# Second stage of a vision tower kernel: patch sums in four column groups, last network product by quarters, key-value sums earlier

## The chip, the cores and the metric

The kernel runs on one core of a Trainium2 chip. The core's engines are PE (TensorE, matmuls from the on-chip memory SBUF into the accumulators PSUM), DVE (VectorE), ACT (ScalarE), POOL (GpSimd) and SP (which here only issues DMA transfers). They run on their own and meet at semaphores. The metric is the device time of one execution in microseconds, the median of several runs. The profile is one further execution, taken with the hardware profiler.

## The reference

```python
def _performer(x, kqv_w, kqv_b, pw, pb, g1, b1, g2, b2, m1w, m1b, m2w, m2b, w):
    h = _ln(x, g1, b1)
    k, q, v = jnp.split(h @ kqv_w.T + kqv_b, 3, axis=-1)
    kp = _prm_exp(k, w)                      # exp(w k - |k|^2 / 2) / sqrt(m), m = 32
    qp = _prm_exp(q, w)
    D = jnp.einsum('btm,bm->bt', qp, kp.sum(axis=1))[..., None]
    kptv = jnp.einsum('btn,btm->bnm', v, kp)
    y = jnp.einsum('btm,bnm->btn', qp, kptv) / (D + EPS)
    y = v + (y @ pw.T + pb)
    h2 = _ln(y, g2, b2)
    return y + jax.nn.gelu(h2 @ m1w.T + m1b, approximate=False) @ m2w.T + m2b

t = _unfold3(x, 1)          # 4 images, 3 channels, 224 x 224: 27 values a token
t = _performer(t, p1...)    # first stage, 50176 tokens of 64 channels an image
t = _unfold3(t, 2)          # 3 x 3 patches with stride 2: 576 values a token
t = _performer(t, p2...)    # second stage, 12544 tokens an image
t = _unfold3(t, 2) @ proj   # 3136 tokens of 768 channels, then a state space layer
...                         # and a layer of experts (the tail)
```

All is in fp32. The change is in the second `_performer`.

## The kernel before

The program has three stages one after the other, with a barrier between: `performer1`, `performer2` (the second stage) and `tail`. Each engine's program is written out by hand as a loop; every engine works its instructions off in that order and waits on semaphores (`after(eng, s, n)` is such a wait that is left out for n of 0 or less).

In the second stage a unit is 448 tokens (4 output rows of 112), 28 units an image, 112 in all. A pair of units is a slot's work: 56 pairs, n = 0 to 55, and the loops run n = 0 to 65. The two units of a pair lie on the two halves of the 128 partitions (64 channels each). The 3 x 3 patches are never written out: the convolutions read strided rows of `xt` and `x4`, and the layer norm over a patch comes in by a mean and a variance that are computed apart.

The first pass over a pair n: SP loads its rows (`load_x`, up to three pairs ahead). ACT squares them (`squares` into `xs`). POOL adds both over the patch's columns and row pairs (`sums`, into `cs` and `css`). PE adds them over the partitions in `statistics` (lines 912 to 922): four matmuls with a constant matrix, the sums of the two units into the two halves of bank 3 (line 917), those of the squares into bank 4 (line 920), 64 columns of the array each, so that every one of 64 partitions holds the same mean. ACT squares the mean from bank 3 into `ms` (line 1113), DVE takes it from bank 4 (line 1228: the variance), ACT makes the inverse deviation `rs` of it by Ln and Exp (lines 1119, 1121). PE convolves to keys and queries (`conv_kq`) and values (`conv_v`), lines 929, 932 and 937; DVE multiplies with `rs` (1238, 1250). One slot later follow `logits` (965, 968), the features (ACT, 1079 and 1083), `transposes` (979, 984), DVE's copy `vt` (1245), and `keys_values` (990): features times values, which DVE adds up over the image in `kvacc` (1263). At the start of an image's second pass `operands`, `matrix` (997, 998) and `weights` make of it the matrices `dw`, `ycw` and `yw`; the latter two are masked by `pm2s` and `pm2` (line 1188) so that a product with the queries picks out the right unit of four. `pm2s` is `pm2` with the two units of the upper 64 partitions (64 to 127) exchanged.

The second pass goes over quads of four units (two pairs; 7 an image, 28 in all, q = 0 to 27), in banks 6 and 7 (`quad_banks`; for some quads of the last image 0 and 1). It has five stages (`second`): 0 the denominator (1022; DVE adds, inverts and multiplies the queries, 1198 to 1202), 1 the centred y (1010, 1004; DVE copies it as `yc`, 1207; ACT squares it, `ycs`, 1091), 2 its variance (1004; ACT Ln and Exp, 1095, 1097), 3 the network's first product (1004; DVE scales, 1212; ACT gelu, 1100), 4 y again (1010) and the network's last product (line 1038), which DVE adds up with a bias and the values as `ob` (line 1217); SP stores it (829). `quads_due` sets when: stages 0 and 1 in one slot, 2, 3 and 4 in the next. So from slot 16 on the even slots hold stages 0 and 1, the odd ones 2 to 4, of the image before; the third image's last quad falls in slots 56 and 57, and the seven quads of the last image in slots 58 to 65, in twos and the last alone, with no convolutions beside them.

A matmul with 64 x 64 weights uses a quarter of the array, one with 128 x 64 half of it, and matmuls on different parts can go side by side. `quadrants` (lines 1000 to 1006) issues four with 64 x 64 weights; for the second of two banks the halves are exchanged (`half[r ^ p]`), so that all four parts of the array are in use.

PE's order in a slot, from line 1041 on: `statistics(n)`, `logits(n - 1)`, at an image's start `matrix`, stages 0 and 2, `conv_kq(n)`, stage 3, `transposes(n - 1)`, `conv_v(n)`, stages 1 and 4, `keys_values(n - 1)`. DVE's: `operands`, variance, `weights`, stage 0, the product `kq`, stage 3, the copy `vt`, the values `vp`, stages 1 and 4, the sum `kvacc`. ACT's: `ms`, features, Ln and Exp of `rs`, `squares(2n + 3)`, stage 2, squares of `kq`, stage 3, `squares(2n + 4)`, stage 1.

Of the kernel before, what the change touches and what calls it, by code (L numbers as in the profile page):

```python
# [21 lines left out]
T = 448  # L22
# [620 lines left out]
def performer2(nc, sem, w, c, t1, t2):  # L643

    with ExitStack() as ctx:
# [15 lines left out]
        def both(q):  # L661
# [8 lines left out]
        bd32 = sb("bd32b", [128, 4, 32])  # L670
        pm2 = sb("pm2", [128, 2, 64])
        pm2s = sb("pm2s", [128, 2, 64])
# [66 lines left out]
                 (srep, c["srep"]), (jb, c["jb64"]), (bd32, c["bd32"].rearrange("p (a m) -> p a m", a=4)),  # L739
                 (pm2, c["pm2"]), (pm2s, c["pm2s"]), (c64, c["c64"]), (c64bd, c["c64bd"]), (c64dup, c["c64dup"]),  # L740
                 (eps64, c["eps64"]), (wa, w["wa2"]), (wb, w["wb2"]), (wf2, w["wf2"]), (ga, w["ga2"]),
# [139 lines left out]
        def _(pe):  # L881
# [30 lines left out]
            def statistics(n):  # L912
                after(pe, s_va, n)
                after(pe, s_vt, n - 1)
                pe.wait_ge(s_cs, 2 * n + 2)
                for g in range(2):
                    mm(ps[half[g], 3, 0:T], ones576[:, 0:64], cs[:, (2 * n + g) % 4, 0:TR2, :], start=True, stop=True)
                pe.wait_ge(s_css, 2 * n + 2)
                for g in range(2):
                    last = mm(ps[half[g], 4, 0:T], ones576[:, 0:64], css[:, (2 * n + g) % 4, 0:TR2, :],  # L920
                              start=True, stop=True)
                last.then_inc(s_st, 1)
# [90 lines left out]
            def second(stage, q):  # L1013
# [20 lines left out]
                if stage == 4:  # L1034
                    pe.wait_ge(s_gl, q + 1)
                    from_q(q, yw)
                    for p in range(2):
                        last = mm(bank(quad_banks(q) + p), m2[:, :], gl[:, u, p, :], start=False, stop=True)
                    last.then_inc(s_o, 1)

            for n in range(LAST):
                if n < NP:
                    statistics(n)
                if 1 <= n <= NP:
                    logits(n - 1)
                if n > BP and n % BP == 1 and n <= NP + 1:
                    matrix(n // BP - 1)
                for stage, q in quads_due(n, (0, 2)):
                    second(stage, q)
                if n < NP:  # L1050
                    conv_kq(n)
                for stage, q in quads_due(n, (3,)):
                    second(stage, q)
                if 1 <= n <= NP:
                    transposes(n - 1)
                if n < NP:
                    conv_v(n)
                for stage, q in quads_due(n, (1, 4)):
                    second(stage, q)
                if 1 <= n <= NP:  # L1060
                    keys_values(n - 1)

        @block.scalar
        def _(act):
# [43 lines left out]
            for n in range(LAST):  # L1108
                u = n % 2
                if n < NP:  # L1110
                    act.wait_ge(s_st, n + 1)
                    after(act, s_va, n - 1)
                    fn(ms[:, u, :], bank(3), ACT.Square).then_inc(s_ms, 1)
                if 1 <= n <= NP:
                    features(n - 1)
                if n < NP:
                    act.wait_ge(s_va, n + 1)
                    after(act, s_vn, n - 1)
                    fn(rs[:, u, :], ms[:, u, :], ACT.Ln, bias=eps64[:, :]).then_inc(s_lv, 1)
                    act.wait_ge(s_lv, n + 1)  # L1120
                    fn(rs[:, u, :], rs[:, u, :], ACT.Exp, scale=-0.5).then_inc(s_rs, 1)
                    squares(2 * n + 3)
# [18 lines left out]
        def _(dve):  # L1141
# [42 lines left out]
            def weights(b):  # L1184
                dve.wait_ge(s_mp, b + 1)
                ts(kps[:, b % 2:b % 2 + 1], ps[:, 2, 128:129], 1.0 / M, None, ALU.mult).then_inc(s_kps, 1)
                for dst, lo, mask in ((ycw, 64, pm2s), (yw, 0, pm2)):
                    nc.vector.scalar_tensor_tensor(dst[:, b % 2], ps[:, 2, lo:lo + 64].unsqueeze(1)
                                                   .to_broadcast([128, 2, 64]), 1.0 / M, mask[:, :, :], ALU.mult,
                                                   ALU.mult).then_inc(s_yw, 1)  # L1190
# [3 lines left out]
            def second(stage, q):  # L1194
# [18 lines left out]
                if stage == 4:  # L1213
                    at = 2 * q % RV
                    dve.wait_ge(s_o, q + 1)
                    after(dve, s_t2[u], 64 * (q // 2))
                    nc.vector.scalar_tensor_tensor(ob[:, u], both(q), bo[:, :], vp[:, at:at + 2, :], ALU.add,
                                                   ALU.add).then_inc(s_ob, 1)

            for n in range(LAST):  # L1220
# [5 lines left out]
                if n < NP:  # L1226
                    dve.wait_ge(s_ms, n + 1)
                    tt(ms[:, u, :], bank(4), ms[:, u, :], ALU.subtract).then_inc(s_va, 1)
                if first:
# [16 lines left out]
                if n < NP:  # L1246
# [3 lines left out]
                    tt(vp[:, n % RV, :], bank(2), rs[:, u, :], ALU.mult).then_inc(s_vn, 1)  # L1250
                for stage, q in quads_due(n, (1, 4)):
                    second(stage, q)
                if 1 <= n <= NP:
# [3 lines left out]
                    for g in range(2):  # L1257
# [3 lines left out]
                        else:  # L1261
                            dve.wait_ge(s_kva, 2 * (n - 1))
                            tt(kvacc[half[g], b % 2, :], kvacc[half[g], b % 2, :], kv, ALU.add).then_inc(s_kva, 1)


# [1065 lines left out]
```

## Time and profile before

| | us |
|---|---|
| median of 3 runs | 8061.27 (8054.65 to 8067.14) |
| the profiled execution's own time | 8056.0 |
| its span | 8054.2 |
| first stage | 0 to about 1784 |
| second stage, 56 slots with convolutions | about 1831 to 2971 |
| second stage, the last eight quads | 2971 to about 3110 |
| tail | about 3113 to 8054 |

| engine | busy us of the span | share |
|---|---|---|
| PE | 7205.3 | 89% |
| DVE | 6156.8 | 76% |
| POOL | 5546.6 | 69% |
| ACT | 4377.1 | 54% |

Busy shares over the whole span mix three stages. To read the second stage, take windows inside it, then the timeline of one odd and one even slot: where a row begins, and which row of another engine ended just before. The rows' ends of matmuls are modelled and overlap the next start, so distances between starts are used for PE.

### The profile page before, as it was taken

What the parts mean: (1) busy time and instruction counts of PE and PEld (TensorE: products, weight loads), DVE (VectorE), ACT (ScalarE), POOL (GpSimd) and SP (SyncE); (2) the same over time, 40 slices, a digit from 0 to 9 for tenths busy, and PEclk for the clock granted to TensorE, in tenths of its full rate; (3) what the DMA queues carried; (4) which work ended last, traced back from release to release, by engine and by line L of the source; (5) the groups of instructions that cost most, each with busy time, mean ns of one, the idle gap of its engine ahead of it and who ended that gap; (6) DMA issues with size and microseconds to landing.
All of it is one profiled execution on the core that took longest, in us unless ns stands there. A gap on an engine that the chain in (4) does not pass through costs nothing.

```text
span 8054.2 us, 87036 instructions
## 1 busy us (share of the span) xinstructions
PE 7205.3 (89%) x31060; PEld 2876.3 (36%) x31060; DVE 6156.8 (76%) x6517; ACT 4377.1 (54%) x7837; POOL 5546.6 (69%) x2487
## 2 busy tenths in 40 slices
PE   8999999979999995689889898898888988988888
PEld 6444444323443431133333333333333333333323
DVE  2566666761333333999999999999999999999995
ACT  3566666763344442555555555555555555555553
POOL 0011111128766640999999999999999999999994
PEclk9999999989999997799899999899998999989988
DMA  1111111125545423333333333333334333334331
GB/s 40 33 46 45 42 44 43 42 60 114 105 98 109 100 61 84 101 116 113 131 130 125 112 119 125 126 124 126 119 109 136 122 128 113 117 128 132 125 110 56
DMA packets 358649, 786.32 MB, mean 98 GB/s; under 512 B 72229, under 2 KB 284727, under 8 KB 350729
## 3 DMA queue, kind: packets, MB, share of 16 engines
q1 hardware_dynamic: 320838, 689.44, 29.1%
q0 software_dynamic: 21712, 51.75, 2.5%
q10 hardware_dynamic: 15666, 39.57, 1.4%
q8 instruction: 246, 4.03, 0.2%
q14 instruction: 187, 1.52, 0.1%
HBM read 597.06 MB, written 183.35 MB: 97 GB/s over the span
## 4 chain that ended last, share of the span: by engine, by line
DVE 34%; issue 13%; ACT 7%; PE 6%; POOL 1%; DMA 0%; DVEq 0%; SPq 0%; ACTq 0%
DVE v L2052 16%; DVE v L2061 15%; ACT ps L1935 2%; PE ps L1672 2%; DVE dl L2042 1%; PE ps L1674 1%; PE ps L1667 1%; ACT dl L1880 1%; ACT gm L1964 1%; PE ps L1802 1%; PE ps L1681 1%; PE ps L1736 1%; ACT dl L1885 0%; ACT L1965 0%; ACT L1964 0%
## 5 line engine op out<-in xcount | busy, mean ns | idle before, releaser
L2061 DVE TENSOR_TENSOR_SCAN v<-ps,v 128x901 f32<-128x901 f32 x1344 | 2732.3, 2033 | 93.4 <-DVE v L2052 0.9
L1636 POOL TENSOR_TENSOR v<-v,ct 128x1792 f32<-128x1792 f32 x672 | 2258.2, 3360 | 288.8 <-ACT st L1896 285.6
L1624 POOL TENSOR_TENSOR v<-xr,bt 128x1792 f32<-128x1792 f32 x672 | 2258.2, 3361 | 65.8 <-DMA bt<-bc_rows 65.8
L1935 ACT ACTIVATE ps<-dr,aa 128x448 f32<-128x448 f32 x2688 | 1596.0, 626 | 1087.4 <-DVE v L2061 1077.7
L2052 DVE SCALAR_TENSOR_TENSOR v<-ps,aa,v 128x448 f32<-128x448 f32 x2688 | 1686.2, 669 | 11.5 <-ACT ps L1935 5.4
L236 POOL DMA_DIRECT2D tokens<-ob x448 | 235.3, 532 | 1533.5 <-DVE ob L563 1490.5
L1736 PE MATMUL ps<-v,dg 128*32 128x448 f32 x5376 | 779.3, 617 | 476.9 <-POOL v L1636 251.8
L1802 PE MATMUL ps<-w_or_w,gm 128*112 128x384 f32 x1792 | 692.4, 534 | 67.8 <-DVE gm L2127 65.0
L1896 ACT ACTIVATE st<-v 128x4 f32<-128x4 f32 x672 | 140.7, 209 | 912.5 <-DVE v L2061 910.6
L1672 PE MATMUL ps<-x,wpa 128*128 128x448 f32 x1008 | 479.0, 613 | 85.9 <-ACT h L1859 75.1
L1667 PE MATMUL ps<-h,w_or_w 128*128 128x448 f32 x1344 | 538.3, 551 | 9.7 <-DVE bcs L2036 9.7
L1802 PEld LDWEIGHTS ps<-w_or_w,gm 128*112 128x112 f32 x1792 | 331.3, 193 | 439.8 <-issue 121.6
L1674 PE MATMUL ps<-x,wpb 64*128 64x448 f32 x1008 | 450.5, 578 | 0.0
L1736 PEld LDWEIGHTS ps<-v,dg 128*32 128x32 f32 x5376 | 136.1, 113 | 856.7 <-POOL v L1636 375.1
L929 PE MATMUL ps<-xt,wa 128*64 128x448 f32 x2016 | 435.0, 565 | 0.0
L552 DVE COPY ht<-ps 112x512 f32<-112x512 f32 x112 | 77.4, 691 | 466.6 <-ACT kp L433 466.6
L1667 PEld LDWEIGHTS ps<-h,w_or_w 128*128 128x128 f32 x1344 | 251.4, 192 | 294.0 <-issue 264.5
L1238 DVE TENSOR_TENSOR kq<-ps,rsa 128x896 f32<-128x896 f32 x56 | 61.1, 1092 | 358.7 <-PE ps L937 337.5
L586 DVE RECIPROCAL qpn<-qpn 128x448 f32<-128x448 f32 x112 | 330.7, 2953 | 3.8
L1672 PEld LDWEIGHTS ps<-x,wpa 128*128 128x128 f32 x1008 | 190.9, 201 | 338.8 <-issue 230.5
L290 PE MATMUL ps<-wki,h 128*112 128x256 f32 x896 | 277.3, 391 | 1.9 <-DVE hu L544 1.9
L1674 PEld LDWEIGHTS ps<-x,wpb 64*128 64x128 f32 x1008 | 174.7, 186 | 271.0 <-issue 271.0
(331 smaller groups left out, 11534.1 us busy)
## 6 DMA issues: line engine op xcount, KB each, us to landing
xr<-h_by_channel SPq DMA_DIRECT2D x168, 896.0 KB, 5.0
dr<-delta_by_channel SPq DMA_DIRECT2D x168, 896.0 KB, 4.7
x<-tokens SPq DMA_DIRECT2D x252, 224.0 KB, 5.3
tokens<-ob POOLq DMA_DIRECT2D x448, 112.0 KB, 2.4
w_or_w<-in_w SPq DMA_DIRECT2D x29, 1536.0 KB, 6.4
w_or_w<-centred_w SPq DMA_DIRECT2D x27, 1536.0 KB, 9.1
h_by_channel<-h SPq DMA_DIRECT2D x112, 336.0 KB, 5.1
delta_by_channel<-dl SPq DMA_DIRECT2D x224, 168.0 KB, 2.8
```

The costliest lines, as they stand in the source:

```text
L586: nc.vector.reciprocal(qpn[:, u % 3, :], qpn[:, u % 3, :]).then_inc(s_dr, 1)
L929: mm(ps[half[g], o, 0:T], wa[:, j, cols], xt[:, 2 * (n % 3) + g, 0:TR2, j:j + 2 * S2 - 1:2], start=(j == 0), stop=False)
L1624: tt(v[:, n % RING, :, 2:T + 2], xr[:, dc % 2, :].rearrange("p (i t) -> p i t", i=4), bt[:, q:q + 1, :].to_broadcast([128, 4, T]), ALU.mul ...
L1636: tt(v[:, n % RING, :, 2:T + 2], v[:, n % RING, :, 2:T + 2], ct[:, q:q + 1, :].to_broadcast([128, 4, T]), ALU.mult).then_inc(s_cm, 1)
L1667: last = mm(into, weights(dc), h[:, i % 3, dc, :], start=(dc == 0), stop=(dc == DC - 1))
L1672: mm(into, even(j), x3[:, 0:TR3, j:j + 2 * S3 - 1:2], start=(j == 0), stop=False)
L1674: return mm(into, odd(j - 3), x3[0:64, 1:TR3 + 1, j - 3:j - 4 + 2 * S3:2], start=False, stop=(j == 5))
L1736: last = mm(ps[32 * g:32 * g + 32, YB, 0:T], dg[:, 4 * k + g, :], v[:, n % RING, g, 2:T + 2], start=(q == 0), stop=False)
L1802: mm(into[:, 0:D // 2], gm[:, m, cs], w2[:, m, lo:lo + D // 2], start=(m == 0), stop=False)
L1935: fn(decay(g), dr[:, dc % 2, g, :], ACT.Exp, scale=aa[:, 4 * k + g:4 * k + g + 1]).then_inc(s_a, 1)
L2052: stt(row, decay(g), aa[:, 4 * k + g:4 * k + g + 1], row, ALU.subtract, ALU.mult).then_inc(s_wt, 1)
L2061: nc.vector.tensor_tensor_scan(row, flat[:, 1024 * pair + 1:1024 * pair + GW + T + 2], row, 0.0, ALU.mult, ALU.add).then_inc(s_sc, 1)
```

## The change

Three things, all in the second stage:

- `statistics` waits for both sums first and then issues its four matmuls with 32 columns each, into the four quarters (32 partitions each) of bank 3: the means of the two units in partitions 0 to 31 and 32 to 63, the means of squares in 64 to 95 and 96 to 127. ACT's square and DVE's difference work on 64 partitions, and ACT's Ln is issued four times, 32 partitions each, to spread the two variances over the 128 partitions of `rs`; the Exp waits for all four.
- The network's last product goes by `quadrants` with the 64 x 64 blocks of `m2` (which is block-diagonal) in place of two matmuls with 128 x 128. Its second bank so holds the two units on exchanged halves; `yw` is masked with `pm2s` to match, `pm2` and its load are gone, and DVE adds up `ob` in three instructions in place of one: 448 elements on 128 partitions for the first bank, then twice 448 on 64 partitions for the second.
- `keys_values(n - 1)` on PE and the sum `kvacc` on DVE stand ahead of stages 1 and 4 in the slot, not behind.

```diff
--- before.py
+++ after.py
@@ -668,7 +668,6 @@
         srep = sb("srep2", [128, 128])
         jb = sb("jb64b", [128, 128])
         bd32 = sb("bd32b", [128, 4, 32])
-        pm2 = sb("pm2", [128, 2, 64])
         pm2s = sb("pm2s", [128, 2, 64])
         c64 = sb("c64", [64, 64])
         c64bd = sb("c64bd", [128, 128])
@@ -737,7 +736,7 @@
 
         loads = [(ident, c["ident"]), (ones576, c["ones576"]), (sqk, c["sqk"]), (dd64, c["dd64"]),
                  (srep, c["srep"]), (jb, c["jb64"]), (bd32, c["bd32"].rearrange("p (a m) -> p a m", a=4)),
-                 (pm2, c["pm2"]), (pm2s, c["pm2s"]), (c64, c["c64"]), (c64bd, c["c64bd"]), (c64dup, c["c64dup"]),
+                 (pm2s, c["pm2s"]), (c64, c["c64"]), (c64bd, c["c64bd"]), (c64dup, c["c64dup"]),
                  (eps64, c["eps64"]), (wa, w["wa2"]), (wb, w["wb2"]), (wf2, w["wf2"]), (ga, w["ga2"]),
                  (gb, w["gb2"]), (ba, w["ba2"]), (bb, w["bb2"]), (kqb, w["kqb2"]), (vb, w["vb2"]), (pb, w["pb2"]),
                  (pw, w["pw2"]), (prj[:, 0:64], w["pwt2"]), (m1, w["m1bd2"]), (m2, w["m2bd2"]), (g2, w["g22"]),
@@ -913,12 +912,12 @@
                 after(pe, s_va, n)
                 after(pe, s_vt, n - 1)
                 pe.wait_ge(s_cs, 2 * n + 2)
-                for g in range(2):
-                    mm(ps[half[g], 3, 0:T], ones576[:, 0:64], cs[:, (2 * n + g) % 4, 0:TR2, :], start=True, stop=True)
                 pe.wait_ge(s_css, 2 * n + 2)
-                for g in range(2):
-                    last = mm(ps[half[g], 4, 0:T], ones576[:, 0:64], css[:, (2 * n + g) % 4, 0:TR2, :],
-                              start=True, stop=True)
+                for k, data in enumerate((cs, css)):
+                    for g in range(2):
+                        at = 64 * k + 32 * g
+                        last = mm(ps[at:at + 32, 3, 0:T], ones576[:, 0:32], data[:, (2 * n + g) % 4, 0:TR2, :],
+                                  start=True, stop=True)
                 last.then_inc(s_st, 1)
 
             def taps(n, o):
@@ -1034,9 +1033,7 @@
                 if stage == 4:
                     pe.wait_ge(s_gl, q + 1)
                     from_q(q, yw)
-                    for p in range(2):
-                        last = mm(bank(quad_banks(q) + p), m2[:, :], gl[:, u, p, :], start=False, stop=True)
-                    last.then_inc(s_o, 1)
+                    quadrants(q, m2, lambda p, r: gl[half[r], u, p, :], False).then_inc(s_o, 1)
 
             for n in range(LAST):
                 if n < NP:
@@ -1055,10 +1052,10 @@
                     transposes(n - 1)
                 if n < NP:
                     conv_v(n)
+                if 1 <= n <= NP:
+                    keys_values(n - 1)
                 for stage, q in quads_due(n, (1, 4)):
                     second(stage, q)
-                if 1 <= n <= NP:
-                    keys_values(n - 1)
 
         @block.scalar
         def _(act):
@@ -1110,14 +1107,16 @@
                 if n < NP:
                     act.wait_ge(s_st, n + 1)
                     after(act, s_va, n - 1)
-                    fn(ms[:, u, :], bank(3), ACT.Square).then_inc(s_ms, 1)
+                    fn(ms[half[0], u, :], ps[half[0], 3, 0:T], ACT.Square).then_inc(s_ms, 1)
                 if 1 <= n <= NP:
                     features(n - 1)
                 if n < NP:
                     act.wait_ge(s_va, n + 1)
                     after(act, s_vn, n - 1)
-                    fn(rs[:, u, :], ms[:, u, :], ACT.Ln, bias=eps64[:, :]).then_inc(s_lv, 1)
-                    act.wait_ge(s_lv, n + 1)
+                    for at in range(0, 128, 32):
+                        of = slice(at // 64 * 32, at // 64 * 32 + 32)
+                        fn(rs[at:at + 32, u, :], ms[of, u, :], ACT.Ln, bias=eps64[of, :]).then_inc(s_lv, 1)
+                    act.wait_ge(s_lv, 4 * (n + 1))
                     fn(rs[:, u, :], rs[:, u, :], ACT.Exp, scale=-0.5).then_inc(s_rs, 1)
                     squares(2 * n + 3)
                 for stage, q in quads_due(n, (2,)):
@@ -1184,7 +1183,7 @@
             def weights(b):
                 dve.wait_ge(s_mp, b + 1)
                 ts(kps[:, b % 2:b % 2 + 1], ps[:, 2, 128:129], 1.0 / M, None, ALU.mult).then_inc(s_kps, 1)
-                for dst, lo, mask in ((ycw, 64, pm2s), (yw, 0, pm2)):
+                for dst, lo, mask in ((ycw, 64, pm2s), (yw, 0, pm2s)):
                     nc.vector.scalar_tensor_tensor(dst[:, b % 2], ps[:, 2, lo:lo + 64].unsqueeze(1)
                                                    .to_broadcast([128, 2, 64]), 1.0 / M, mask[:, :, :], ALU.mult,
                                                    ALU.mult).then_inc(s_yw, 1)
@@ -1214,8 +1213,12 @@
                     at = 2 * q % RV
                     dve.wait_ge(s_o, q + 1)
                     after(dve, s_t2[u], 64 * (q // 2))
-                    nc.vector.scalar_tensor_tensor(ob[:, u], both(q), bo[:, :], vp[:, at:at + 2, :], ALU.add,
-                                                   ALU.add).then_inc(s_ob, 1)
+                    stt = nc.vector.scalar_tensor_tensor
+                    stt(ob[:, u, 0], bank(quad_banks(q)), bo[:, :], vp[:, at, :], ALU.add, ALU.add)
+                    for r in range(2):
+                        last = stt(ob[half[r], u, 1], ps[half[1 - r], quad_banks(q) + 1, 0:T], bo[half[r], :],
+                                   vp[half[r], at + 1, :], ALU.add, ALU.add)
+                    last.then_inc(s_ob, 1)
 
             for n in range(LAST):
                 u = n % 2
@@ -1225,7 +1228,7 @@
                     operands(image)
                 if n < NP:
                     dve.wait_ge(s_ms, n + 1)
-                    tt(ms[:, u, :], bank(4), ms[:, u, :], ALU.subtract).then_inc(s_va, 1)
+                    tt(ms[half[0], u, :], ps[half[1], 3, 0:T], ms[half[0], u, :], ALU.subtract).then_inc(s_va, 1)
                 if first:
                     weights(image)
                 for stage, q in quads_due(n, (0,)):
@@ -1248,8 +1251,6 @@
                     if n >= RV:
                         dve.wait_ge(s_ob, (n - RV) // 2 + 1)
                     tt(vp[:, n % RV, :], bank(2), rs[:, u, :], ALU.mult).then_inc(s_vn, 1)
-                for stage, q in quads_due(n, (1, 4)):
-                    second(stage, q)
                 if 1 <= n <= NP:
                     b, r = divmod(n - 1, BP)
                     dve.wait_ge(s_kv, n)
@@ -1261,6 +1262,8 @@
                         else:
                             dve.wait_ge(s_kva, 2 * (n - 1))
                             tt(kvacc[half[g], b % 2, :], kvacc[half[g], b % 2, :], kv, ALU.add).then_inc(s_kva, 1)
+                for stage, q in quads_due(n, (1, 4)):
+                    second(stage, q)
 
 
 S3 = S2 // 2
```

## Rows read from the trace of the kernel before

**Rows 1.** Busy time by window, second stage (engines' busy us, clock, DMA).

```profile
core 0: us, PE busy (x) PEld busy (x) DVE busy (x) ACT busy (x) POOL busy (x), PEclk, DMA share, GB/s
...
2115.00:2395.00 280.00, 280.00 (x1557) 112.42 (x1554) 99.87 (x122) 125.13 (x169) 191.97 (x158) 1.00 0.52 105
...
2955.00:3020.00 65.00, 46.26 (x232) 17.84 (x229) 27.94 (x33) 24.05 (x26) 0.00 (x0) 0.87 0.06 14
3020.00:3115.00 95.00, 59.00 (x202) 17.08 (x200) 39.63 (x32) 27.42 (x27) 1.80 (x8) 0.70 0.15 36
```

**Rows 2.** Timeline of an odd slot, PE: start us, us, engine, line, operation, count.

```profile
2499.74 0.97 PE L917 MATMUL ps<-cs,ones 128*64 128x448 f32 x4
...
2519.44 1.10 PE L990 MATMUL ps<-vt 112*128 112x64 f32 x8
...
2520.47 0.97 PE L917 MATMUL ps<-cs,ones 128*64 128x448 f32 x4
...
2521.27 0.92 PE L920 MATMUL ps<-css,ones 128*64 128x448 f32 x4
...
2522.03 0.92 PE L965 MATMUL ps<-kq,wf 128*64 128x448 f32 x4
...
2523.63 0.98 PE L1004 MATMUL ps<-ycs,jb64b 64*64 64x448 f32 x8
...
2524.54 2.61 PE L929 MATMUL ps<-xt,wa 128*64 128x448 f32 x12
...
2531.91 0.93 PE L1004 MATMUL ps<-yc,m1g 64*64 64x448 f32 x8
...
2539.98 1.77 PE L1038 MATMUL ps<-gl,m2bd 128*128 128x448 f32 x4
...
2541.58 1.00 PE L990 MATMUL ps<-vt 112*128 112x64 f32 x8
...
2542.52 0.97 PE L917 MATMUL ps<-cs,ones 128*64 128x448 f32 x4
```

**Rows 3.** Timeline, PE in the tail: line 1736 and what follows.

```profile
5019.53 0.96 PE L1736 MATMUL ps<-v,dg 128*32 128x448 f32 x8
5020.42 1.02 PE L1740 MATMUL ps<-h,ident 128*128 128x448 f32 x2
```

**Rows 4.** Timeline, a slot with no second pass: key-value product and its sum.

```profile
1898.88 1.10 PE L990 MATMUL ps<-vt 112*128 112x64 f32 x8
...
1900.02 0.40 DVE L1263 TENSOR_TENSOR kvacc<-kvacc,ps 64x32 f32<-64x32 f32 x2 [0.40 <-PE ps L990]
```

**Rows 5.** Timeline of the same odd slot as rows 2: DVE and ACT.

```profile
2519.57 1.15 DVE L1207 TENSOR_SCALAR yc<-ps,by 128x896 f32<-128x896 f32 x1 [1.26 <-PE ps L1004]
...
2520.76 0.95 ACT L1091 ACTIVATE ycs<-yc 128x896 f32<-128x896 f32 x1 [4.49 <-DVE yc L1207]
...
2525.15 0.67 ACT L1119 ACTIVATE rsa<-ms,eps64b 128x448 f32<-128x448 f32 x1
...
2527.49 1.01 ACT L1095 ACTIVATE rs<-ps,eps64b 128x896 f32<-128x896 f32 x1
...
2541.79 1.15 DVE L1217 SCALAR_TENSOR_TENSOR ob<-ps,bo,v_pairs 128x896 f32<-128x896 f32 x1 [2.02 <-PE ps L1038]
```

**Rows 6.** The page's costliest groups: count, busy us, mean ns, idle before.

```profile
L2052 DVE SCALAR_TENSOR_TENSOR v<-ps,aa,v 128x448 f32<-128x448 f32 x2688 | 1686.2, 669 | 11.5 <-ACT ps L1935 5.4
```

**Rows 7.** Timeline, start of an image's second pass (slot 29): DVE and PE.

```profile
2393.22 0.96 DVE L1182 TENSOR_SCALAR rows<-rowr,ksum 128x129 f32<-128x129 f32 x1
...
2394.62 0.49 PE L997 MATMUL ps<-rr,kvr 128*128 128x129 f32 x2
```

**Rows 8.** Timeline of the drain, slots 56 and 57: DVE and PE.

```profile
2978.74 0.95 DVE L1245 COPY vt<-ps 112x768 f32<-112x768 f32 x1
...
2978.87 1.70 PE L1010 MATMUL ps<-q_quads,ycw 64*128 64x448 f32 x4 [2.56 <-DVE q_quads L1202]
...
2980.51 1.77 PE L1004 MATMUL ps<-v_pairs,c64bd 64*64 64x448 f32 x8
...
2992.46 3.35 PE L1038 MATMUL ps<-gl,m2bd 128*128 128x448 f32 x4
```

## The prediction

> **What bounds the kernel now.** The change touches only the second of three stages, so I first cut the span in windows. The second stage runs from about 1784 to 3110 us. In its 56 slots with convolutions PE is busy 280.00 of 280 us at full clock, while in the same window DVE is busy 100, ACT 125 and POOL 192 [rows 1]. An engine busy all the time still has to be shown to be the bound: in the timeline of one slot each group of matmuls starts where the one before it can let it start, and the waits of ACT and DVE are for PE [rows 2]. So until 2971 us a slot lasts as long as PE's list of groups, and what PE saves there is saved in the time, as long as nobody else comes late. After it the last eight quads drain (2971 to 3110 us): PE is only partly busy, at clock 0.87 and 0.70, and a chain through DVE, ACT and PE sets the time [rows 1].
>
> I count a group of matmuls by the distance from its start to the start of the next group, since the ends in the rows are modelled. A fp32 matmul of 448 columns stands in the trace as two records of about 0.375 us each.
>
> **Part 1, statistics in four column groups.** Before, the two matmuls on `cs` and the two on `css` take 2522.03 - 2520.47 = 1.56 us: two column groups side by side, one pair after the other [rows 2]. After, all four lie side by side. The nearest row is the tail's line 1736, the same form (128 rows, 32 columns, 448 moved, one bank, four groups): 8 records in 5020.42 - 5019.53 = 0.89 us [rows 3]. What comes next, the logits, has 64 columns, and a change of the array's division costs: the first group after one takes 0.80 where the next takes 0.76 (2520.47, 2521.27, 2522.03 [rows 2]), 0.05 more. The 0.89 already has the change of form at its end. So 0.89 + 0.05 = 0.94 in place of 1.56: **0.62 us per slot**, times 55 slots = 34 us. The first slot runs with PE just woken and behind POOL; I take 0.5 to 1 us there, from the halved work and one load less (`pm2`). The wait for `css` now stands ahead of the products on `cs` as well, and all of PE's list behind it; POOL is a slot ahead from the third slot on, so only the first two can feel it.
>
> The bounds: if the four streams went only two at a time, the group would stay at 1.56 plus the extra change of form (0.05 + 0.14), a loss of 0.2 per slot; if the switch were free, 0.75, a gain of 0.8 per slot. I take the row of line 1736 because it is the same form at the same clock.
>
> The Trainium skill, page "TensorEngine Tiling (Array Packing)", section "Key Properties", says that a change of tiling mode drains the engine. That speaks against this part, since it adds one change per slot. By this rule the trace agrees, and its price is inside the 0.89 and the 0.05.
>
> **Part 2, the last product by quarters.** Before, two 128x128 matmuls (line 1038) take 2541.58 - 2539.98 = 1.60 us and are followed by the key-value sums (line 990) with no change of form, 2542.52 - 2541.58 = 0.94 us: together 2.54 [rows 2]. After, the order is line 990, line 1010, quarters, next statistics. Quarters of this form (line 1004, 8 records) take 2524.54 - 2523.63 = 0.91; line 990 with changes of form on both sides takes 2520.47 - 2519.44 = 1.03 [rows 2]. Together 1.94, so **0.60 us less per quad**. 19 quads end inside the convolving slots: 11 us. Masking `yw` with `pm2s` changes no form.
>
> **Part 3, key-value sums ahead.** For PE it is the same work with the same number of changes of form where a slot has stage 1, so 0. Its wait is for `vt`, copied by DVE some 4 us earlier behind a whole conv_v; it doesn't bind while there are convolutions. DVE's accumulation comes before DVE's last operation of the slot. In a slot with no second pass nothing moves: there the accumulation starts at 1900.02 and takes 0.40, and the logits, which wait for it, would now start at about 1898.88 + 1.03 + 0.89 = 1900.80 [rows 4]. 0.38 us is left for the semaphore. It fits.
>
> **What the other engines pay, and whether it shows.** I put t0 at the start of the group behind a slot's last PE group, and compare with the next user:
> - ACT, four Ln of 32 partitions for one of 128. One takes 0.67 us for 448 elements [rows 5]; time goes by elements per partition, so at most 2.0 us more per slot (rather less, if they overlap by the 0.1 us that other neighbours do). In the odd slots this lies between stage 1's square `ycs` and the normalised product. `yc` begins 0.13 after t0 and takes 1.15, `ycs` ends at 2521.71 - 2519.44 = 2.27 [rows 5]. Stage 2 on PE would start at t0 + 0.89 + 0.80 + 0.85 = 2.54, where it was 4.19. 0.27 us is left: tight. Further on, stage 2's Ln started at 8.05 and now starts about 2.0 later and 1.4 earlier, 8.65, ends at 9.66; PE's line 1004 on `yc` needs it at 12.47 - 1.65 = 10.8, less 0.4 for its weights. 0.8 us is left. The normalisation for `kq` ends before all this and isn't near its user.
> - DVE, three scalar_tensor_tensor of 448 for one of 896 (1.15 us). Nearest row: line 2052, same operation, 448 elements, PSUM input, 0.669 us [rows 6]. 3 x 0.67 = 2.0, so 0.86 more. PE's stage 0 of the next quad waits for it: done at t0 + 0.13 + 2.01 = 2.14, needed at 2.54. 0.4 us is left.
> - SP: `store` waits for the same result and the x-loads queue behind it; they go out about 1.6 us later in every second slot. I book nothing for it; should the loads land late, it is a case of rival 1.
> - POOL's sums: 192 of 280 us [rows 1], and the later squares have several us to spare.
> - At the start of an image (slots 15, 29, 43) PE's `matrix` waits for DVE's `rows`. That ended at 2394.18 and PE came at 2394.62 [rows 7]; PE now comes 1.65 earlier and DVE, rid of only 0.4, does not. I book about 0.9 us each, **-2.7 us**.
>
> **The drain.** Slot 56 begins straight behind slot 55's quarters: line 990 no longer stands there, 1.5 us less, but stage 0 then waits for DVE's three pieces, which leaves 0.9. In slot 56 the key-value sums now wait for the `vt` copy, which ends at 2979.69, ahead of stage 1, which had started at 2978.87: it starts after line 990, about 2981.0, **-2.1 us** [rows 8]. From there, for each quad that the chain passes, the product gets shorter (3.35 us at the low clock to the 1.77 of line 1004's quarters; 1.6 to 0.9 at the high one [rows 2, 8]) and DVE longer by 0.86: +0.7 in slot 57, about +1.0 for each of three pairs, about 0 for the last. Sum of the drain: 0.9 - 2.1 + 0.7 + 3.0 = **+2.5 us**.
>
> **The sum.** 34 + 0.7 + 11 - 2.7 + 2.5 = 46 us. From the profiled execution's 8056.0 us that makes 8010; the median of the runs shown lies 5.3 us above it, and since the tail's other 4940 us are not touched, I carry that over: 8061.3 - 46 = **8015 us**.
>
> **The rivals.**
> 1. The small margins (0.27, 0.4, 0.38 us) are not enough, and a new wait takes part of the gain: PE waits in each slot. If each of the 55 slots lost 0.4 us, 22 us would go, and the time would be 8037. Against it: an engine takes up what another has done within 0.04 us (DVE to ACT, 2520.72 to 2520.76) to 0.13 us (PE to DVE) in these rows [rows 5]. Chance 0.22, 8023 to 8041.
> 2. Four column groups don't run side by side in this place, where they read four buffers that POOL has written, and go in pairs: part 1 then costs 0.2 x 55 = 11 us, part 2 gives 11, start and drain give 3 and the image starts take 3, so 0 in all, 8061. Against it: line 1736 [rows 3]. Chance 0.04.
> 3. Two quarters on different row halves can't write one bank at a time, so that the last product stays at 1.6 and only part 1 is left: 46 - 11 - 4 = 31, 8030. Rows of line 1004 speak against it: 0.91 for 8 records means that the halves went together, and it writes the same bank in just this pattern [rows 2]. The Trainium skill states that rule, "TensorEngine Tiling (Array Packing)", section "Gotcha 1: PSUM Pressure". Chance 0.02.
> 4. Slower: ACT. If each of the four small Ln took much longer than a large one, the odd slots' chain ycs, Ln x4, Exp, squares, Ln would reach PE late. The margin is 0.8 us and the gain to eat is 46 us over 20 odd slots, 2.3 each; so the four would have to cost 3.1 us over my 2.7, that is 1.45 us each in place of 0.67. With 1.7 us each the loss would be 20 x (4.1 - 0.8) = 66 us, and the time 8081. No row hints at it. Chance 0.03.
> 5. More is gained than counted (switches cheaper, small idles between groups gone): 55 to 60 us, 8001 to 8006. Chance 0.08.
>
> **How the numbers follow.** My forecast, 8007 to 8023, has 0.58; the rest of 0.03 is drift of the tail. The range of 8 in 10 takes in the forecast, most of rival 1, rival 3 and half of rival 5: 8002 to 8039. A difference under 0.2% (16 us) can't be told from none by these measurements. Faster than 8045 are the forecast and rivals 1, 3, 5: 0.90, less a little for drift, 0.89. Within: rival 2 and the worst of 1: 0.08. Slower: 0.03.
>
> **What would show it.** In the profile after: the statistics group of 8 records with 0.89 us to the logits; line 990 then line 1010 then 8 records of the last product, 0.91 us; slots with no second pass 0.62 us shorter, pairs of later slots of 40.9 us in place of 2542.52 - 2499.74 = 42.8 [rows 2]; PE still at 280 of 280. Four Ln of 0.66 and three DVE pieces of 0.67. Wrong would be: idle time of PE ahead of the logits, stage 2 or stage 0 with a releaser on DVE or ACT, or a group of statistics over 1.1 us.

## The result

The changed kernel takes 8015.43 us (median of 4 runs, 8013.76 to 8024.47), the kernel before in the same comparison 8062.83 us (4 runs, 8054.65 to 8067.14): a ratio of 0.9944 with a 95% interval of 0.9931 to 0.9957, so 47 us or 0.56% less. Run again in a later comparison, five times, it took 8010.73 against 8053.38, ratio 0.9947 (0.9935 to 0.9960). The forecast was 8015 us, 8002 to 8039.

The total says little about where. The profiled execution of the changed kernel happened to be the slowest of its four (8024.47 us), and its tail, which the change doesn't touch, took 4954 us where it took 4938 to 4944 in every other profile of this study. So I compare the second stage alone: from POOL's first instruction in it (the memset of `ob`) to POOL's first one in the tail. That is 3112.85 - 1783.62 = 1329.2 us before and 3068.62 - 1781.30 = 1287.3 after, **41.9 us less**; in the second profile of the changed kernel 1284.5, 44.7 less. The kernel before and each experiment have one profile only, so a difference of 2 or 3 us between two stages is no more than these two profiles of one kernel show.

The windows of the changed kernel, with the columns of [rows 1]: engines' busy time, clock, DMA.

```profile
2105.00:2345.00 240.00, 240.00 (x1417) 93.18 (x1413) 90.96 (x114) 138.15 (x190) 170.55 (x141) 1.00 0.52 107
...
2925.00:2954.00 29.00, 17.43 (x83) 7.35 (x80) 13.02 (x21) 7.86 (x9) 0.00 (x0) 0.67 0.07 16
2954.00:3063.00 109.00, 68.73 (x294) 16.77 (x294) 58.62 (x56) 36.91 (x36) 0.00 (x0) 0.71 0.13 30
```

In this window PE is still busy all the time: what it got rid of went straight into the time. Only where it takes in an image start is a little missing (279.49 of 280 us from 2115 to 2395). ACT went from 125 of 280 us to 138 of 240, and no wait for it shows on PE. Here is the timeline of an odd slot and of the start of the next, PE, DVE and ACT (start us, us, engine, line, operation, shapes, count, idle before and releaser). It answers to [rows 2, 5].

```profile
2492.20 0.98 PE L1003 MATMUL ps<-v_pairs,c64bd 64*64 64x448 f32 x8
...
2493.11 0.57 PE L919 MATMUL ps<-cs,ones 128*32 128x448 f32 x2
2493.13 0.57 PE L919 MATMUL ps<-css,ones 128*32 128x448 f32 x2
...
2493.25 1.15 DVE L1206 TENSOR_SCALAR yc<-ps,by 128x896 f32<-128x896 f32 x1 [1.49 <-PE ps L1003]
...
2494.00 0.97 PE L964 MATMUL ps<-kq,wf 128*64 128x448 f32 x4
...
2494.44 0.95 ACT L1088 ACTIVATE ycs<-yc 128x896 f32<-128x896 f32 x1 [3.95 <-DVE yc L1206]
2494.80 0.92 PE L967 MATMUL ps<-kqs,sqk 128*64 128x448 f32 x4
...
2495.66 0.98 PE L1003 MATMUL ps<-ycs,jb64b 64*64 64x448 f32 x8
...
2497.18 2.75 ACT L1118 ACTIVATE rsa<-ms,eps64b 32x448 f32<-32x448 f32 x4
...
2501.59 1.01 ACT L1092 ACTIVATE rs<-ps,eps64b 128x896 f32<-128x896 f32 x1
...
2503.93 0.93 PE L1003 MATMUL ps<-yc,m1g 64*64 64x448 f32 x8
...
2511.05 1.10 PE L989 MATMUL ps<-vt 112*128 112x64 f32 x8
...
2512.08 1.02 PE L1009 MATMUL ps<-q_quads,yw 64*128 64x448 f32 x4
...
2513.03 0.98 PE L1003 MATMUL ps<-gl,m2bd 64*64 64x448 f32 x8
2513.95 0.57 PE L919 MATMUL ps<-cs,ones 128*32 128x448 f32 x2
...
2514.08 0.68 DVE L1217 SCALAR_TENSOR_TENSOR ob<-ps,bo,v_pairs 128x448 f32<-128x448 f32 x1 [1.49 <-PE ps L1003]
...
2514.78 1.38 DVE L1219 SCALAR_TENSOR_TENSOR ob<-ps,bo,v_pairs 64x448 f32<-64x448 f32 x2
...
2516.49 1.02 PE L1021 MATMUL ps<-q_quads,dw 128*128 128x448 f32 x2
```

The statistics' four streams start within 0.02 us of each other and the logits follow 2494.00 - 2493.11 = 0.89 us later; the logits' first group takes 0.80. The last product by quarters takes 2513.95 - 2513.03 = 0.92 where line 1038 took 1.60. The slot lasts 2513.95 - 2493.11 = 20.84 us.

Slot lengths by kind (medians of the distances between the first statistics record of one slot and of the next, in us) and the parts of the stage. "To the statistics" is from the stage's start to slot 0's, "drain" from slot 55's statistics to the tail. The rows e1 to e8 are the experiments below.

| kernel | to the statistics | slot 0 | no second pass | even | odd | image starts (15, 29, 43) | drain | stage |
|---|---|---|---|---|---|---|---|---|
| before | 47.5 | 15.42 | 17.76 | 20.73 | 22.04 | 18.61, 22.69, 22.68 | 163.9 | 1329.2 |
| changed | 47.9 | 15.12 | 17.18 | 20.12 | 20.83 | 18.20, 22.07, 22.45 | 164.3 | 1287.3 |
| e5, the same again | 47.9 | 15.13 | 17.18 | 20.12 | 20.83 | 18.18, 21.99, 21.76 | 162.2 | 1284.5 |
| e1, statistics only | 48.3 | 15.10 | 17.18 | 20.11 | 21.43 | 18.18, 22.07, 22.09 | 163.5 | 1296.5 |
| e2, quarters only | 47.4 | 15.18 | 17.76 | 20.99 | 21.44 | 18.59, 22.09, 22.09 | 163.6 | 1322.1 |
| e3, order only | 47.3 | 15.22 | 17.76 | 20.73 | 22.23 | 18.59, 23.18, 22.88 | 166.7 | 1335.5 |
| e4, statistics and quarters | 47.9 | 15.12 | 17.18 | 20.99 | 20.86 | 18.18, 21.47, 21.47 | 162.0 | 1299.9 |
| e6, eight Ln | 47.9 | 15.12 | 17.18 | 20.12 | 22.37 | 18.26, 22.37, 22.37 | 162.6 | 1311.9 |
| e7, four DVE pieces | 47.9 | 15.11 | 17.18 | 20.60 | 20.83 | 18.18, 22.47, 22.14 | 168.4 | 1300.6 |
| e8, order back at image ends | 47.9 | 15.11 | 17.18 | 20.12 | 20.83 | 18.18, 22.21, 21.76 | 160.7 | 1283.2 |

### The profile page after: what moved, and what is told of

Same layout as the page of the kernel before. It is cut to its first block, busy times and chain, and to the rows that moved or that the text cites. A ratio compares the mean times of both kernels' runs of the same rounds, so it can differ in the third digit from the quotient of the medians.

```text
span 8022.7 us, 87538 instructions
## 1 busy us (share of the span) xinstructions
PE 7160.5 (89%) x31172; PEld 2842.9 (35%) x31172; DVE 6187.2 (77%) x6573; ACT 4485.1 (56%) x8005; POOL 5541.3 (69%) x2487
## 3 DMA queue, kind: packets, MB, share of 16 engines
q14 instruction: 189, 1.54, 0.1%
## 4 chain that ended last, share of the span: by engine, by line
DVE 34%; issue 13%; ACT 7%; PE 7%; POOL 1%; DMA 0%; DVEq 0%; ACTq 0%; SPq 0%
DVE v L2055 16%; DVE v L2064 15%; ACT ps L1938 2%; PE ps L1675 2%; DVE dl L2045 1%; PE ps L1677 1%; PE ps L1670 1%; ACT dl L1883 1%; ACT gm L1967 1%; PE ps L1805 1%; PE ps L1684 1%; PE ps L1739 1%; ACT dl L1888 0%; ACT L1968 0%; ACT L1967 0%
```

## The experiments

The questions left open: whether the two savings of PE add up as the sum has them, what the third part does (I had booked it at nothing among the convolutions), and how far ACT and DVE are from being the bound, on which two of the rivals rested.

### e1, the statistics alone

From the kernel before, `statistics`, `ms`, the variance and the four Ln as in the change, nothing else.

> Part 1 alone (statistics in four column groups with its four Ln); last product and order as before. My theory, by the sums: 0.615 us in each of 54 or 55 slots, 33 to 34 us; against it some 2 us at three image starts, where PE now waits for DVE's rows, and at most 0.1 us in each odd slot, where the logits come to within 0.1 us of the key-value sum, which still stands behind DVE's out sum. Stage shorter by 30 to 32 us. Rival (small margins fail): PE idle ahead of stage 2 in odd slots, 20 us or less in all. Rival (streams go in pairs): longer than before by 10 us.

8021.22 us against 8056.44, ratio 0.9959 (0.9945 to 0.9973); stage 32.8 us shorter, a little more than expected. Slots with no second pass, even slots and odd ones are all 0.58 to 0.62 us shorter, and among them PE waits neither for ACT nor for DVE. The surplus over the 30 to 32 us expected lies where I had booked 2 us of loss: the image starts 29 and 43 gained 0.62 and 0.59 us like any other slot.

### e2, the quarters alone

```diff
-                    for p in range(2):
-                        last = mm(bank(quad_banks(q) + p), m2[:, :], gl[:, u, p, :], start=False, stop=True)
-                    last.then_inc(s_o, 1)
+                    quadrants(q, m2, lambda p, r: gl[half[r], u, p, :], False).then_inc(s_o, 1)
```

and with it `pm2s` for `yw` and the out sum in three pieces.

> Part 2 alone (last product by quarters, DVE's out sum in three pieces); statistics and order as before. My theory: 0.59 us less for each of 19 quads in slots with convolutions, 11 us; the key-value sum on DVE ends 2.5 us after the quarters and the logits start 2.6 after, so no stall; in the drain, after the last convolution, about 0, since DVE's 0.92 us more is on the chain there and the shorter product pays for it. Stage shorter by 9 to 12 us. Rival (DVE's pieces are the bound): PE idle ahead of the logits or stage 0, gain under 5 us.

8045.88 us against 8056.44, ratio 0.9988 (0.9979 to 0.9997); stage 7.2 us shorter, less than the 9 to 12 expected. The odd slots have their 0.60, but the even ones got 0.26 us longer. The timeline at the start of an even slot shows it (the columns as above):

```profile
2492.83 1.10 PE L989 MATMUL ps<-vt 112*128 112x64 f32 x8
2492.97 0.69 DVE L1215 SCALAR_TENSOR_TENSOR ob<-ps,bo,v_pairs 128x448 f32<-128x448 f32 x1 [1.26 <-PE ps L1003]
2493.67 1.38 DVE L1217 SCALAR_TENSOR_TENSOR ob<-ps,bo,v_pairs 64x448 f32<-64x448 f32 x2
...
2494.67 0.92 PE L919 MATMUL ps<-css,ones 128*64 128x448 f32 x4
2495.08 2.42 SPq L828 DMA_DIRECT2D tokens<-ob  x4
2495.08 0.40 DVE L1264 TENSOR_TENSOR kvacc<-kvacc,ps 64x32 f32<-64x32 f32 x2
...
2495.63 0.97 PE L964 MATMUL ps<-kq,wf 128*64 128x448 f32 x4
```

The key-value sum stands behind DVE's three pieces and ends at 2495.48, and the logits start 0.15 us after it, 0.96 us behind line 919 where 0.75 was usual. I had it end 0.1 us ahead of the logits; the pieces take 2.08 us, not 2.01, and don't overlap.

### e3, the order alone

```diff
+                if 1 <= n <= NP:
+                    keys_values(n - 1)
                 for stage, q in quads_due(n, (1, 4)):
                     second(stage, q)
-                if 1 <= n <= NP:
-                    keys_values(n - 1)
```

and the same on DVE.

> Part 3 alone (key-value sums ahead of stages 1 and 4 on PE and DVE); the rest as before. My theory: one more change of the array's form in each slot with stage 4, since the 128-wide last product now stands between others: about 0.19 us for 19 quads, 3.7 us; and in slot 56 the second pass waits for the vt copy and the sums at a low clock, 2.8 us. Longer than before by 5 to 7 us, which in the total is near what can't be told apart; the slots in the trace tell. Rival (prediction's text, order costs nothing among convolutions): odd slots 22.05 us as before.

8064.33 us against 8056.44, ratio 1.0009 (1.0000 to 1.0017); stage 6.3 us longer. The odd slots are 0.19 us longer and the drain 2.8 us: both as expected. The 0.19 stands in the timeline of an odd slot:

```profile
2536.42 1.10 PE L990 MATMUL ps<-vt 112*128 112x64 f32 x8
2537.46 1.02 PE L1010 MATMUL ps<-q_quads,yw 64*128 64x448 f32 x4
2538.41 1.77 PE L1038 MATMUL ps<-gl,m2bd 128*128 128x448 f32 x4
2540.11 0.97 PE L917 MATMUL ps<-cs,ones 128*64 128x448 f32 x4
```

Line 990 takes 1.04 us to the next start and line 1038 takes 1.70, where they took 0.94 and 1.60 as neighbours in [rows 2].

### e4, statistics and quarters with the old order

> Parts 1 and 2 without part 3 (order as before). My theory: DVE adds the key-value sum behind three pieces, ending 2.5 us after the quarters, while the logits that wait for it could start 1.92 after: 0.7 us of stall in each of 19 odd slots, 13 us; slot 56 gets back 2 us. Stage shorter than before by about 30 us where the whole change brings 42: part 3, worth nothing by itself, is what keeps parts 1 and 2 from getting in each other's way. Rival (PE is the bound and order is free): within 3 us of the whole change, 42 us.

8024.12 us against 8056.44, ratio 0.9960 (0.9947 to 0.9972); stage 29.3 us shorter. The even slots take 20.99 us where the whole change gives 20.12. The timeline names the wait:

```profile
2478.36 1.10 PE L989 MATMUL ps<-vt 112*128 112x64 f32 x8
...
2480.61 0.40 DVE L1266 TENSOR_TENSOR kvacc<-kvacc,ps 64x32 f32<-64x32 f32 x2
...
2481.15 0.97 PE L964 MATMUL ps<-kq,wf 128*64 128x448 f32 x4 [0.81 <-DVE kvacc L1266]
```

PE idles 0.81 us ahead of the logits, until 0.14 us after DVE's `kvacc`. This is the point of the third part. By itself it costs 6.3 us; beside the other two it is worth 12.6 us (1299.9 to 1287.3) or, by the second profile of the changed kernel, 15.4. It gives 0.87 us in each of 19 even slots, 16.4 in all, and gives some of it back at the image starts and in the drain. The three parts alone sum to 32.8 + 7.2 - 6.3 = 33.7 us, together they bring 41.9 or 44.7.

### e5, the changed kernel again

> The changed kernel itself once more, as the mark for the other three of this series. My theory: second stage 1287 us as in its first profile, tail about 4941 us as in all other profiles (the 4954 of its first profile was that execution's own), so a profiled time near 8012. Rival (the change alters the tail): tail again over 4950 us.

8010.73 us against 8053.38. The profiled execution took 8005.64, its tail 4940 us. The 13 to 14 us that the first profile's tail took longer were its own. This pair of profiles of one kernel also shows what two executions differ by inside the stage: nothing in ordinary slots, 0.7 us in slot 43, 2 us in the drain.

### e6, eight Ln

```diff
-                    for at in range(0, 128, 32):
+                    for k, at in enumerate((0, 32, 64, 96, 0, 32, 64, 96)):
                         of = slice(at // 64 * 32, at // 64 * 32 + 32)
-                        fn(rs[at:at + 32, u, :], ms[of, u, :], ACT.Ln, bias=eps64[of, :]).then_inc(s_lv, 1)
-                    act.wait_ge(s_lv, 4 * (n + 1))
+                        dst = rs[at:at + 32, u, :] if k > 3 else spare[at:at + 32, :]
+                        fn(dst, ms[of, u, :], ACT.Ln, bias=eps64[of, :]).then_inc(s_lv, 1)
+                    act.wait_ge(s_lv, 8 * (n + 1))
```

> The changed kernel with eight Ln of 32 partitions for the four; the four more write to a buffer that nobody reads. In the changed kernel's trace stage 2's Ln ends 0.94 us before PE loads the weights of the product that waits for it (2502.60 and 2503.54). My theory: four more Ln take 2.75 us, so PE waits 1.8 us in each of the 20 odd slots, plain and even slots stay (their Ln and Exp end over 3 us ahead of their user): stage longer by 36 us than the changed kernel's. By the prediction's own margin of 0.8 us: 39 us. Rival (ACT is not near the path): no difference. Rival (ACT bounds every slot): 55 times 2.75, 150 us.

8036.37 us against 8053.38, ratio 0.9978 (0.9969 to 0.9987); stage 27.3 us longer than e5's. Only slots with stages 2 to 4 pay, as the theory of one chain in the odd slots has it. But it is 1.54 us and not 1.8 in each of the 17 ordinary ones, and the image starts 29 and 43 pay only 0.4 and 0.6, since PE waited there already; so it is 27 us and not 36.

```profile
2519.74 1.01 ACT L1093 ACTIVATE rs<-ps,eps64b 128x896 f32<-128x896 f32 x1
...
2520.80 0.98 PE L1004 MATMUL ps<-yc,m1g 64*64 64x448 f32 x8 [1.31 <-ACT rs L1093]
```

The product starts 0.05 us after the Ln that it waits for. I had taken off the time of a weight load that runs ahead of the product; on a late release load and product start together (both at 2520.80 here; at 2503.54 and 2503.93 in the changed kernel). In the changed kernel the Ln ends at 2502.60 and the product starts at 2503.93, so its margin is 2503.93 - 2502.60 - 0.05 = 1.28 us, and 4 x 0.69 less 1.28 is 1.48, near the 1.54.

### e7, four pieces of the out sum

```diff
-                    stt(ob[:, u, 0], bank(quad_banks(q)), bo[:, :], vp[:, at, :], ALU.add, ALU.add)
+                    for r in range(2):
+                        stt(ob[half[r], u, 0], ps[half[r], quad_banks(q), 0:T], bo[half[r], :],
+                            vp[half[r], at, :], ALU.add, ALU.add)
```

> The changed kernel with the out sum's first piece (128 partitions) cut in two of 64, so four DVE pieces of 0.69 us. In the changed kernel's trace the third piece ends 0.33 us before stage 0 starts on PE. My theory: of these 0.33 some 0.15 to 0.25 are the semaphore, so nearly all of the 0.69 shows: 0.5 to 0.6 us in each of the 20 even slots, 11 us, and 3 us more in the drain; stage longer by 12 to 15 us. By the prediction's margin of 0.4 us: 0.29 a slot, 9 us with the drain. Rival (DVE is hidden): 3 us or less.

8027.67 us against 8053.38, ratio 0.9967 (0.9955 to 0.9980); stage 16.1 us longer than e5's. Even slots are 0.48 us longer, and stage 0 waits with DVE as its releaser:

```profile
2479.01 1.38 DVE L1221 SCALAR_TENSOR_TENSOR ob<-ps,bo,v_pairs 64x448 f32<-64x448 f32 x2
...
2480.54 0.99 PE L1021 MATMUL ps<-q_quads,dw 128*128 128x448 f32 x2 [0.45 <-DVE ob L1221]
```

It starts 0.15 us after the last piece. Of the changed kernel's 0.33 us (2516.16 to 2516.49 in its odd slot's timeline) 0.18 were free: one more DVE piece of any size that matters in this place costs. The drain cost 6 us rather than 3; nine outputs fall in it, and nine times 0.69 would be 6.2, an estimate.

### e8, the old order where an image ends

Line 989 and the sum `kvacc` stand behind the second pass again in the slots with n % 14 == 0, ahead of it in all others:

```diff
-                if 1 <= n <= NP:
+                if 1 <= n <= NP and n % BP:
                     keys_values(n - 1)
                 for stage, q in quads_due(n, (1, 4)):
                     second(stage, q)
+                if 1 <= n <= NP and n % BP == 0:
+                    keys_values(n - 1)
```

> The changed kernel with the key-value sums behind the second pass again, on PE and DVE, in slots 14, 28, 42 and 56 alone, where an image's first pass ends. My theory: in slot 56 stage 1 no longer waits for the vt copy and a product at the low clock, 2 to 2.6 us back, and slots 29 and 43 lose PE's wait ahead of the matrix product, 0.6 and 1.0 us back: stage shorter by 3.5 to 4.5 us, below what the total can tell, to be seen in the trace. Rival (the drain's loss comes from the clock alone and not from the order): 1.6 us or less.

8006.20 us (8003.40 to 8010.73) against 8053.38, ratio 0.9942 (0.9929 to 0.9954), beside 8010.73 (8005.64 to 8017.22) for the changed kernel on the same chip; five runs each, and the ranges overlap. Its stage is 1283.2 us, 1.3 and 4.1 less than the changed kernel's two. The smaller of these would fit the rival too (1.6 or less), so the stage doesn't decide and the timeline must. Half of the theory held. In slot 56 the second pass starts on `q_quads` again and not on the copy `vt`. These are the rows of the changed kernel,

```profile
2932.80 0.95 DVE L1248 COPY vt<-ps 112x768 f32<-112x768 f32 x1
2933.81 1.97 PE L989 MATMUL ps<-vt 112*128 112x64 f32 x8 [3.43 <-DVE vt L1248]
2935.70 1.87 PE L1009 MATMUL ps<-q_quads,ycw 64*128 64x448 f32 x4
```

and these of e8:

```profile
2931.13 0.95 DVE L1262 COPY vt<-ps 112x768 f32<-112x768 f32 x1
2931.27 1.87 PE L1009 MATMUL ps<-q_quads,ycw 64*128 64x448 f32 x4 [2.56 <-DVE q_quads L1203]
```

From `dn` to `yc` of that quad it takes 7.78 us where the changed kernel takes 10.43 and 10.72 and the kernel before 7.80. But 0.7 to 1.0 us of it is given back by the end of slot 57 (15.31 us from `yc` to `ob`, against 14.57 and 14.26); why is open. The other half fell: slots 29 and 43 didn't get shorter (22.21 and 21.76). Their wait is of another kind, below. As a version it is the best of the study by its median; the difference to the changed kernel is under what these runs can tell.

## Why the prediction was right, and where it wasn't

- **Statistics, 0.62 us a slot.** Right: 0.89 and 0.80 in place of 0.80, 0.76 and 0.75; slots 0.58 to 0.61 us shorter. Line 1736 of the tail was the right row to price it by: the same form took the same 0.89 us. Rival 2 (streams in pairs) is out.
- **Quarters, 0.60 us a quad.** Right in the whole change: odd slots lost 1.21 us, even ones 0.61, the pair came to 40.95 us where 40.9 was forecast. Rival 3 is out as well: quarters on both row halves wrote one bank side by side in 0.92 us, so the rule that this rival rests on doesn't hold here, where they write different halves of the bank's partitions.
- **The order, 0.** Wrong as a price, right in the sum. The step compared PE's groups only in the finished change, where it cancels in slots with stage 1 and is inside Part 2's sum in the others. e3 shows 0.19 us an odd slot, and e4 what the text didn't see at all: without it, DVE's three pieces would have stood between the key-value product and the logits and eaten 13 to 15 us. I had looked for the waits that the change adds, not for the one it keeps away.
- **The margins.** 0.27 us ahead of stage 2 was exact: `ycs` ends at 2495.39, PE starts at 2495.66. 0.4 us ahead of stage 0 was 0.33, of which 0.15 is the time from DVE's end to PE's start (e7). 0.38 ahead of the logits in slots with no second pass was exact too. The 0.8 ahead of line 1003 on `yc` was 1.28; it was sized too small mainly because the 0.4 us of a weight load was taken off. Rival 1 needed these to fail; none did, and e7 shows that it was near in one place and e6 that it was not in the other. ACT's wait for its x-loads went up to 59.1 us in all, where it had been 15.2, without PE waiting for ACT. That fits SP's later loads, but no part does it alone (20.7 to 27.0 us in e1 to e3), nor the first two together (23.5 in e4).

```profile
ACT xs L1069 <- DMA x<-tokens: 59.1, 18, 4.6
```

- **Image starts, -2.7 us.** The sum over slots 15, 29 and 43 is -1.8 in the first profile and -1.0 in the second. It had no place for slot 15: nothing moves in slot 14, which has no second pass, so PE came 0.62 us earlier and not 1.65, and it lost only 0.2. Slots 29 and 43 lost 0.3 to 1.0 each.
- **The start, +0.7.** Wrong, it was about 0 (to the statistics 0.4 us more, slot 0 0.3 less). Before, PE did the half on `cs` while POOL still worked at `css`; now the whole waits for POOL. Slot 0's convolutions do start 1.0 us sooner after the stage's start, but slot 1 gives it back, where PE has to wait for `css` and didn't before:

```profile
1844.32 0.57 PE L919 MATMUL ps<-cs,ones 128*32 128x448 f32 x2 [0.85 <-POOL css L868]
```

- **The drain, +2.5 and slot 55's 0.62.** From slot 55's statistics on, 3.1 us less were forecast; it is 0.3 more in one profile and 1.7 less in the other. The term that was mis-sized most is slot 56: line 989 ran at a granted clock of 0.50 (1.2 GHz) there, 1.89 us between starts and not 1.1 (the rows above), so the order cost 2.6 to 2.9 us in that slot and not 2.1. The three pairs brought 1.1 and 3.0 us against 3.0 forecast, and groups on the path differ in clock from one execution to the next: slot 57's product on `ycs` took 1.31 us in the first profile and 0.98 in the second.
- **The sum.** 46 us were forecast for the stage, 41.9 and 44.7 measured, and 47.4 and 42.7 between the medians of the totals. That the forecast met the first median to within half a microsecond is luck: the stage gained 1 to 4 us less than forecast, and the spread of the totals made up for it. The ordinary slots were not luck.

## What to carry to other kernels

Where one engine is busy without a gap, price an edit by distances between starts of the same form elsewhere in the trace, with the change of form at both ends, and the slots come out to a few hundredths. Then list for every wait of that engine how much time its releaser has left: the change gave its full gain because a third part, a loss by itself, moved a small sum out of the way of a wait that the other two would have laid bare. Before taking such a part for idle, or out, measure the parts together.

## What the runs showed of the hardware that was not expected

DVE's small preparations at an image's start take very different times. `rows`, a tensor_scalar of 128x129 from SBUF to SBUF, took 0.96 us in [rows 7], 1.38 in slot 29 of e5,

```profile
2368.62 1.38 DVE L1181 TENSOR_SCALAR rows<-rowr,ksum 128x129 f32<-128x129 f32 x1
```

and 0.29 in slot 57 of the changed kernel, where POOL has nothing to do any more:

```profile
2940.43 0.29 DVE L1181 TENSOR_SCALAR rows<-rowr,ksum 128x129 f32<-128x129 f32 x1
```

In e8 the copy `kvr` before it took 1.14 us beside POOL and 0.23 without. The Trainium skill, page "SBUF — State Buffer", section "SBUF: two separate sides", says that DVE and GpSimd share one pair of ports, which a DVE instruction takes in some of its modes, and that the one that comes second waits for the whole instruction of the other. By this rule the spread agrees: POOL's instructions take 1.1 to 1.4 us there, and in all 30 image starts of the ten traces at which POOL works `rows` ended 0.08 to 0.15 us behind the end of one of them. No run shows in which mode `rows` ran. So PE's wait in slots 29 and 43 depends on where POOL happens to be, which would explain why slot 43 took 22.45 us in one profile of the changed kernel and 21.76 in the other, and why e8's order didn't shorten it. e4 has e8's order around these slots and shows the other case: `kvr` took 0.59 and 0.23 us, `rows` ended 0.10 and 0.52 us before PE came, and both slots took 21.47. No run here took POOL's work away, so the cause is argued from the rows, not shown by an experiment.
